# Router logits in four column groups of TensorE, and a stream's first scan read from PSUM

## What is computed

```
h1 = elu(segment_sum(softmax_by_dst(leaky(es[src] + ed[dst])) * z[src]))   # streams 0, 1 (and 2 on z2)
H = gelu(layernorm(x) @ W1 + b1)              # 6250 x 1024, all in fp32
probs = softmax(H @ Wg + bg)                  # 8 experts
assign = argmax(probs)
out = x + probs[assign] * (H @ Wd[assign] + bd[assign])
```

## Time and profile before

| | us |
|---|---|
| median of 3 runs | 5587.15 |
| lowest, highest | 5586.58, 5588.17 |
| the profiled execution, its own time | 5590.89 |
| its span (first to last instruction) | 5588.9 |

### The profile page before, as it was taken

One profiled execution on the slowest core, in us unless ns is written; L12 is line 12 of the kernel. 1 busy time (PEld: TensorE's weight loads), 2 busy tenths in 40 slices (PEclk: granted clock), 3 DMA queues, 4 the chain that ended last, 5 costly groups with the idle time before them and its releaser, 6 DMA issues.

```text
span 5588.9 us, 75596 instructions
## 1 busy us (share of the span) xinstructions
PE 4056.0 (73%) x18105; PEld 2830.9 (51%) x18105; DVE 3567.1 (64%) x10862; ACT 2783.9 (50%) x5993; POOL 3285.7 (59%) x3443
## 2 busy tenths in 40 slices
PE   3997776666662596577777776578777776797998
PEld 3554554544442595355555554456555554333565
DVE  5377766666667666577777776677777786622111
ACT  2365666666662232477777776544444442343222
POOL 0124777777774755677777776477777777012222
PEclk9998878778875598799888987798999998898999
DMA  4293555455541344445444444344444444200110
GB/s 129 67 280 102 144 140 140 138 140 140 140 131 48 108 139 128 138 135 135 135 136 136 136 136 115 109 131 133 133 133 133 133 133 129 86 23 28 34 34 27
DMA packets 349460, 658.87 MB, mean 118 GB/s; under 512 B 80930, under 2 KB 198704, under 8 KB 348760
## 3 DMA queue, kind: packets, MB, share of 16 engines
q0 software_dynamic: 156336, 433.90, 28.6%
q1 hardware_dynamic: 182928, 211.64, 12.8%
q10 hardware_dynamic: 9772, 8.50, 0.5%
HBM read 539.67 MB, written 115.45 MB: 117 GB/s over the span
## 4 chain that ended last, share of the span: by engine, by line
PE 20%; POOL 16%; issue 16%; DVE 9%; DMA 8%; ACT 1%; DVEq 1%; POOLq 0%; SPq 0%; ACTq 0%
POOL AR L1001 11%; DMA AR<-D_z,SRCI 7%; PE ps L1229 4%; PE ps L2669 4%; PE ps L2650 4%; PE ps L2357 3%; DVE AR L1088 2%; POOL AR L1685 2%; PE ps L2369 1%; POOL D_sx L1675 1%; DVE AR L1115 1%; POOL AR L1813 1%; DVE AR L1093 1%; PE ps L2273 1%; DMA D_sx<-AR 1%
## 5 line engine op out<-in xcount | busy, mean ns | idle before, releaser
L1001 POOL DMA_INDIRECT AR<-D_z,SRCI x1856 | 1777.5, 958 | 637.0 <-issue 498.1
L1229 PE MATMUL ps<-AR 128*128 128x264 f32 (+2 forms) x5568 | 1706.8, 459 | 359.5 <-DVE AR L1088 140.3
L1229 PEld LDWEIGHTS ps<-AR 128*128 128x128 f32 x5568 | 1209.1, 226 | 690.1 <-issue 286.8
L1001 POOL DMA_INDIRECT AR<-D_h,SRCI x904 | 870.0, 962 | 277.3 <-issue 246.2
L1115 DVE TENSOR_TENSOR AR<-ps,AR 128x264 f32 (+2 forms) x1392 | 588.0, 422 | 161.2 <-DVE AR L1115 136.0
L1276 ACT ACTIVATE AR<-iota_n,NREL 128x128 f32<-128x128 f32 x1856 | 587.6, 389 | 29.6 <-PE ps L1229 26.2
L1093 DVE TENSOR_TENSOR AR<-AR,ps 128x1024 f32<-128x1024 f32 x464 | 558.3, 1203 | 0.1
L1034 DVE TENSOR_TENSOR AR<-AR 128x128 f32<-128x128 f32 (+2 forms) x174 | 49.0, 282 | 674.6 <-SPq L982 674.4
L1287 ACT ACTIVATE AR<-AR,iota_p 128x1024 bf16<-128x1024 bf16 x348 | 394.7, 1134 | 21.0 <-DMA AR<-D_rel 21.0
L1289 ACT ACTIVATE AR<-AR,ones 128x1024 bf16<-128x1024 bf16 x348 | 399.5, 1148 | 11.4
L1293 ACT ACTIVATE AR<-ps 128x128 f32<-128x128 f32 (+2 forms) x174 | 47.1, 271 | 594.2 <-PE ps L1195 589.0
(11 more groups left out here) (446 smaller groups left out, 7700.2 us busy)
## 6 DMA issues: line engine op xcount, KB each, us to landing
AR<-D_rel SPq DMA_DIRECT2D x348, 256.0 KB
D_sx<-AR SPq DMA_DIRECT2D x8, 6370.0 KB
AR<-D_z,SRCI POOLq DMA_INDIRECT x1856
AR<-D_h,SRCI POOLq DMA_INDIRECT x928
D_y<-AR SPq DMA_DIRECT2D x106, 128.0 KB, 1.7
AR<-in_L_ffn_Wd SPq DMA_DIRECT2D x8, 1024.0 KB, 12.2
AR<-D_mask SPq DMA_DIRECT2D x58, 128.0 KB
D_h<-AR SPq DMA_DIRECT2D x49, 132.0 KB, 1.7
```

Source lines behind the costliest of these rows:

```text
L1001: e.indirect_dma_start(out=GV[:, u % 48, :], out_offset=None, in_=D_row[L.i], in_offset=bass.IndirectOffsetOnAxis(ap=SRCI[:, u:u + 1], axi ...
L1229: t = e.matmul(banks[n % 3][:, 0:YW], Sr[:, u % 8, :], GV[:, u % 48, L.GW - YW:L.GW], start=(i == 0), stop=(i == 1))
```

## The change

Two things, in all three streams and in the last routing.

In the streams ACT's copy `turned` goes, and with it the tile TSC and the semaphore `t_there`. The first scan and the last subtraction read the turned scores in PSUM, and the scan waits for TensorE's `t_ps`.

In the routing the eight logits matmuls go to four groups of 32 array columns: strip m writes partitions 32 (m mod 4) to 32 (m mod 4) + 31 of bank 6, with Wg widened to 32 columns per strip (24 of them zero). The four partial sums stay apart. DVE's addition of the bias takes all 128 partitions, and each turn becomes a plain fp32 matmul with all 128 partitions as the weights and a 128x8 matrix `sel`, which has ones where the partition is an expert's in any of the groups, so that it also adds up the four parts. Some tiles move. DVE gets the making of `sel` and of the zeros at the head of the routing, and one copy of the bias in its first round.

```diff
@@ runs @@
-                e.wait_ge(t_there, K + 1)
-                e.tensor_tensor_scan(B1[0:P, :], mk[0:P, 0, :], TSC[0:P, :], -BIG, ALU.add, ALU.max).then_inc(*dv.up())
+                e.wait_ge(t_ps, K + 1)
+                e.tensor_tensor_scan(B1[0:P, :], mk[0:P, 0, :], BK_T[0:P, 0:128], -BIG, ALU.add, ALU.max).then_inc(*dv.up())
@@ reference @@
-                e.tensor_tensor(B2[0:P, :], TSC[0:P, :], B2[0:P, :], ALU.subtract).then_inc(x_ready, 1)
+                e.tensor_tensor(B2[0:P, :], BK_T[0:P, 0:128], B2[0:P, :], ALU.subtract).then_inc(x_ready, 1)
@@ stream_scalar @@
-            def turned(k):
-                e.wait_ge(t_ps, L.k0 + k + 1)
-                e.activation(TSC[0:P, :], BK_T[0:P, 0:128], ACT.Copy).then_inc(t_there, 1)
...
-                if k < NG2:
-                    turned(k)
@@ tiles of the routing @@
-        W1, Wg, b1, bgc, bd, pw1 = AR.take(2, 1024), AR.take(8, 8), AR.take(8), AR.take(2), AR.take(2048), AR.take(72)
+        W1, b1, bgc, bd, pw1 = AR.take(2, 1024), AR.take(8), AR.take(2), AR.take(2048), AR.take(72)
...
-        rl = AR.ring(2, 512)
+        rl, sel, Wg = AR.ring(2, 512), AR.take(8), AR.take(8, 32)
...
-        EX1, RK1, PS1, PI1 = AR.take(NB), AR.take(NB), AR.take(NB), AR.take(NB, dt=I32)
+        EX1, PI1 = AR.take(NB), AR.take(NB, dt=I32)
...
+        RK1, PS1 = keep.take(NB), keep.take(NB)
@@ route_sync @@
-            e.dma_start(Wg[:, :, :], A["L1_ffn_Wg"].rearrange("(m p) n -> p m n", p=128)).then_inc(route_in, 16)
+            e.dma_start(Wg[:, :, 0:8], A["L1_ffn_Wg"].rearrange("(m p) n -> p m n", p=128)).then_inc(route_in, 16)
@@ route_tensor @@
                     for m in range(8):
-                        t = e.matmul(banks[6][0:8, 0:w], Wg[:, m, :], h[:, m, 0:w], start=(m == 0), stop=(m == 7))
+                        c = 32 * (m % 4)
+                        t = e.matmul(banks[6][c:c + 32, 0:w], Wg[:, m, :], h[:, m, 0:w], start=(m < 4), stop=(m >= 4))
...
-                        t = e.transpose(banks[7][:, 8 * i:8 * i + 8], rl[g % 2][0:8, 128 * i:128 * i + 128], ident[0:8, 0:8])
+                        t = e.matmul(banks[7][:, 8 * i:8 * i + 8], rl[g % 2][:, 128 * i:128 * i + 128], sel[:, :], start=True, stop=True)
@@ route_vector @@
+            e.memset(Wg[:, :, 8:32], 0.0)
+            e.memset(bgc[:, 1:2], 0.0)
+            e.tensor_tensor(sel[:, :], ident[:, 0:8], ident[:, 32:40], ALU.add).then_inc(*dv.up())
+            for c in (64, 96):
+                e.wait_ge(*dv.now())
+                e.tensor_tensor(sel[:, :], sel[:, :], ident[:, c:c + 8], ALU.add).then_inc(*dv.up())
...
                     if g == 0:
                         e.wait_ge(route_in, 96)
+                        e.tensor_copy(bgc[0:8, 1:2], bgc[0:8, 0:1]).then_inc(*dv.up())
+                        e.wait_ge(*dv.now())
...
-                    e.tensor_scalar(rl[g % 2][0:8, 0:w], banks[6][0:8, 0:w], bgc[0:8, 0:1], None, ALU.add).then_inc(r_log, 1)
+                    e.tensor_scalar(rl[g % 2][:, 0:w], banks[6][:, 0:w], bgc[:, 1:2], None, ALU.add).then_inc(r_log, 1)
```

More of the change, by code:

```diff
@@ L905, in program @@
         mk_in = [sem(f"mk_in{i}") for i in range(2)]
-        rows_there, oh_ready, ad_ps, e_ready, t_ps, t_there, run_ready, edge_ps, row_ready, col_ps, x_ready, ex_ready, al_ps = [
-            sem(n) for n in ("rows_there", "oh_ready", "ad_ps", "e_ready", "t_ps", "t_there", "run_ready", "edge_ps", "row_ready", "col_ps", "x_ready", "ex_ready", "al_ps")]
+        rows_there, oh_ready, ad_ps, e_ready, t_ps, run_ready, edge_ps, row_ready, col_ps, x_ready, ex_ready, al_ps = [
+            sem(n) for n in ("rows_there", "oh_ready", "ad_ps", "e_ready", "t_ps", "run_ready", "edge_ps", "row_ready", "col_ps", "x_ready", "ex_ready", "al_ps")]
         assert AR.at <= 25608
@@ L922, in program @@
         OHr = AR.ring(2, 1024, dt=BF16)
-        AD, TSC, B1, B2 = [AR.take(128) for _ in range(4)]
+        AD, B1, B2 = [AR.take(128) for _ in range(3)]
         RL, RF, FW, BW = [AR.take(140) for _ in range(4)]
```

## The result

The changed kernel takes 5535.38 us (median of 4 runs, 5533.44 to 5538.4) beside 5587.66 us of the kernel before in the same comparison: 52.3 us less, ratio 0.9904, 95% interval 0.9892 to 0.9916.

The account below looks back on a forecast made before the run. POOL's gathers bound the streams, TensorE the routing. Ten steady rounds save 24.5 us, group 0 saves 2.8, group 1 costs 0.55 and the head 0.9: about 26 us less, 5561 us, range 5536 to 5580.

Parts of the forecast that it names:

- 9 slots: Routing's logits: neighbouring matmuls overlap by one pass, 4.0 us instead of 7.0, saving 3.0 us; chance 0.49.
- starts stay in the order of the list: Routing's logits: TensorE starts matmul passes strictly in program order, so a matmul's second pass holds up those behind it.
- rival: Routing's logits: four column groups run side by side, saving 5.0 us per group, 48 us in all, 5539 us; chance 0.31.
- The drains: Routing's TensorE: changes of tiling mode drain it twice per round, 0.3 us, which would take 3 us from the gain.
- The floor of the range: Routing's logits: at least about 1.9 us, from 16 weight loads one after another (1.5 us) and the last matmul's end.
- The turns: Routing's logit turns: eight passes take 0.96 us, 0.55 more than now in each round; bounds 0.3 and 0.75.
- A steady round: Routing, groups 2 to 11: loses 3.0 us and gains 0.55, so 2.45 us less each, 24.5 us for ten.
- The odd rounds: Routing's first two and last groups: group 0 saves 2.8 us, group 1 costs 0.55, the last group 0.
- the rival's term: Routing's group 0: with four column groups side by side it saves 4.8 us.
- the head: Start of the routing: DVE's two memsets and chain of three additions cost about 0.9 us, counted fully.
- Nothing for the streams, the bias, Wg's load: Streams gain 0, covered by POOL's pace; bias over 128 partitions at most 0.74 us; Wg's load ends before its first use.

Follow-up runs that it names:

- the run with neighbours in one group: Changed kernel with strips 2j and 2j + 1 in column group j, so that every second matmul finds its group taken; ratio to the kernel before 0.9943.
- the run with the split wait: Changed kernel with logits strips 0 to 3 waiting only for the first four gelus, strips 4 to 7 for all eight; ratio to the kernel before 0.9957.
- the streams alone: Kernel before with only the streams' part of the change, without the routing's part; ratio to the kernel before 1.001.

## Why the prediction was wrong

**The step that failed** is the price of the logits: "Eight matmuls then take 9 slots where 16 stood", from the assumption that "starts stay in the order of the list". The slots are 4, the saving 5.1 us (6.96 to 1.86 between the logits' start and the next work) instead of 3.0. The two passes of one matmul don't meet, as said, but they don't have to: the engine starts the other matmuls' first passes ahead of the second ones, and the run with neighbours in one group shows it passing a whole blocked matmul. I weighed a rule against rival there, with nothing in the trace to decide, and gave 0.49 to the one and 0.31 to the other. The in-order rule of the Trainium skill, page "TensorE: Matmul & The Clock Gate", section Part 3, The mechanism, is not what these runs show for starts across column groups. Its other figure, the span of one matmul plus some 4 ns per further tile, comes near when applied to one wave: there the starts are 7 ns apart, and the first wave takes 0.64 us where its single passes take 0.62.

The drains that the prediction priced at 0.3 us per round have something to them, but are no cost of the change. Behind the logits the step is some 0.1 us longer than between weights of 128 columns, in both kernels (0.52 beside 0.43). Ahead of them it is hidden by the wait for the last gelu; in the run with the split wait, where it isn't, the logits start 0.20 us after the last rank pass, where rank passes follow one another after 0.11. Whether the engine drains there or a weight load lies open is not shown.

**The floor of the range.** I had 1.9 us for four side by side, from sixteen weight loads in a row. The value was right (1.92), its reason wasn't: the loads lie side by side as well, and the time is 4 x 0.428 plus the tail of the last matmul. The 48 us of this rival then fell short of 52.3, mostly by the next term.

**The turns** were put at 0.55 us per round and cost 0.17. I took eight passes at 0.12 each, which was near (0.81 us to the next hidden layer), but compared them with the 0.41 us of busy time instead of the 0.54 us to the next work, and didn't see that the turns on 8 partitions also came 0.10 us later behind the row turns. Over ten rounds that is 3.8 us.

**A steady round** was forecast at 21.5 us and is 19.01: 4.96 less instead of 2.45, of which 5.10 less are logits, 0.17 more turns, and 0.03 is rounding and small shifts.

**The odd rounds** went as described in their waits, but not in two sizes. The bias of group 0 moved from 4821.71 to 4815.19, by 6.5 us; taking away the 2.4 that the trace was ahead at the head and adding the head's 0.7 leaves 4.8, the rival's term. Group 1 brought nothing and cost more than 0.55. Its turns are the second row here:

```profile
4843.97 0.66 DVE AR L2549
...
4844.68 1.88 PE ps L2382 x8
4846.55 16.55 PE ps L2352 x32
```

They took 1.88 us instead of 0.59. TensorE had stood idle for DVE before them, 1.3 us here and 1.95 us in the kernel before, and in both kernels the granted clock was then 0.50, the 1.2 GHz level. There the eight passes follow one another after 0.21 us, where it is 0.11 in a steady round, and the four short passes of the kernel before after 0.11, where it is 0.06. So the difference is 1.3 us. I had priced it at the upper level. The first row is the kernel before, the second the changed one:

```profile
4850.00:4854.00 4.00, 2.59 (x7) 1.54 (x8) 2.74 (x15) 2.46 (x4) 2.39 (x3) 0.50 1.06 354
...
4843.00:4849.00 6.00, 4.69 (x13) 2.88 (x12) 3.40 (x23) 3.75 (x6) 3.83 (x4) 0.50 1.07 358
```

From DVE's first operation to the hidden layer of group 2 the changed kernel takes 67.74 us (4778.81 to 4846.55), the kernel before 70.78 (4781.22 to 4852.00), 3.0 less. With the measured terms, 4.8 for group 0, 1.3 for these turns and 0.7 for the head (of 0.9 forecast), the sum is 2.8. From there to the first gather of the experts another 48.7 us went, ten rounds of 4.96 less 0.9. The first of the ten saved 4.6 (from 26.3 to 21.7) and the last 4.5 (from 23.0 to 18.5), which is most of the 0.9. In the last of them only one block's row turn lies between the logits and their turns, and these wait 0.5 us for the bias:

```profile
5036.94 0.75 DVE L2549 TENSOR_SCALAR AR<-ps,AR 128x512 f32<-128x512 f32 x1 [0.47 <-PE ps L2365]
...
5037.75 1.06 PE L2382 MATMUL ps<-AR 128*128 128x8 f32 x8 [0.51 <-DVE AR L2549]
```

**Nothing for the streams, the bias, Wg's load** was right as far as the runs resolve it: ratio 1.001 for the streams alone; the bias over 128 partitions takes 0.75 us, as over 8 (0.74); and the first hidden layer, which waits for the load of Wg, starts 16.4 us after the clearing of ones1 in both kernels.

## What to carry to other kernels

Where there are several matmuls that use 32 or fewer columns of the array, giving them different column groups divides their time by the number of groups; this is shown here for eight fp32 matmuls of 128 partitions and 512 moving columns, with two and four groups, and the order of the list need not be arranged for it. The partial sums cost almost nothing (0.17 us per round here) if a transpose that follows can be a matmul that adds them. Price such an edit from the start of one operation to the start of the next different one, with the gaps, not from its busy time; and look for what waits next, since 0.5 us of waits per round could still be taken away around the logits.

## What the runs showed of the hardware

TensorE overtook blocked matmuls: with strips 0 and 1 in one column group, the first passes of strips 0, 2, 4 and 6 started within 0.05 us. Eight weight loads of 128x32 for four groups took 0.16 us together, 0.11 alone. Eight short passes with weights of 8 or 64 partitions among ones of 128 cost 0.26 us more per round than with 128 partitions (0.98 us to the next work against 0.81, and 0.62 from the last row turn against 0.52). From weights of 128 columns to weights of 32 and back a step was some 0.1 us longer each way (0.20 beside 0.11, 0.52 beside 0.43), with weights of 8 columns as well on the way back. A scan of DVE out of PSUM took the same 0.41 us as out of SBUF.
